# Expert down products in fp32r halves, loop bounds read into registers once, merged matrix split inside the context attention

## The reference, cut to what matters

```python
x = x + tanh(g_xattn[0]) * lag_attention(layernorm(x), ctx, ctx)          # part 1
x = x + tanh(g_ffn[0])   * experts(layernorm(x), gate_w, u, g, d)          # parts 2 and 3
x = x + tanh(g_xattn[1]) * cross_attention(layernorm(x), ctx, Wq, bq, Wk, bk)  # part 4
x = x + tanh(g_ffn[1])   * quantised_ffn(layernorm(x), ...)                # part 5

# experts: 2048 rows of 1024, 16 experts of 112 inner units, two experts for each row
w = weights of the two chosen experts of each row
gate_out, up_out = x @ g.T, x @ u.T          # split by expert
h = silu(gate_out) * up_out
out = einsum('bei,hei,be->bh', h, d_r, w)    # the down product

# cross attention
Q, K = text @ Wq.T + bq, ctx @ Wk.T + bk
out = softmax(Q @ K.T / 32) @ ctx
```

## Time and profile before

| | |
|---|---|
| median of 3 runs | 1354.48 us (1353.6 to 1355.89) |
| the profiled execution, own time | 1356.5 us |
| its span, from the first instruction to the last | 1354.8 us |
| instructions | 20940 |
| PE busy | 1239.7 us, 92% of the span |
| DVE, ACT, POOL busy | 783.7, 513.5, 573.0 us |
| experts: gate and up of tile 0 to the last down product | 598 to 839 us |

### The profile page before, as it was taken

One profiled execution on the slowest core, in us unless ns is written; L12 is line 12 of the kernel. 1 busy time (PEld: TensorE's weight loads), 2 busy tenths in 40 slices (PEclk: granted clock), 3 DMA queues, 4 the chain that ended last, 5 costly groups with the idle time before them and its releaser, 6 DMA issues. The chain is left out here.

```text
span 1354.8 us, 20940 instructions
## 1 busy us (share of the span) xinstructions
PE 1239.7 (92%) x6442; PEld 846.7 (62%) x6442; DVE 783.7 (58%) x2026; ACT 513.5 (38%) x939; POOL 573.0 (42%) x931
## 2 busy tenths in 40 slices
PE   4799999999878999999999998999999999968886
PEld 2354544445435954458888786988888898635443
DVE  3889999998963680015433333444554443369885
ACT  2555545454423400023322222232222322168894
POOL 5667877777642001013221222523212231068884
PEclk8999999999988899999999999999999999879998
DMA  5211212302004502227778874535333331131111
GB/s 197 92 64 32 93 62 96 138 31 109 0 1 149 224 1 84 70 85 246 265 240 283 273 233 161 187 94 128 114 103 124 96 101 54 62 70 47 62 62 78
DMA packets 52481, 156.25 MB, mean 115 GB/s; under 512 B 5952, under 2 KB 16192, under 8 KB 52288
## 3 DMA queue, kind: packets, MB, share of 16 engines
q1 hardware_dynamic: 39152, 113.46, 23.6%
q0 software_dynamic: 13264, 41.95, 10.8%
HBM read 112.93 MB, written 45.61 MB: 117 GB/s over the span
## 5 line engine op out<-in xcount | busy, mean ns | idle before, releaser
L1210 PEld LDWEIGHTS ex_bank<-ex_xT,ex_gu 128*112 128x112 f32 x1248 | 140.4, 177 | 24.3 <-issue 23.3
L1210 PE MATMUL ex_bank<-ex_xT,ex_gu 128*112 128x128 f32 x1248 | 143.6, 273 | 2.0 <-issue 1.0
L44 PE MATMUL xa_bank<-fT_high,M_hi 128*128 128x256 f32 x512 | 144.0, 281 | 0.0
L46 PE MATMUL xa_bank<-fT_high,M_lo 128*128 128x256 f32 x512 | 143.0, 279 | 0.0
L45 PE MATMUL xa_bank<-fT_low,M_hi 128*128 128x256 f32 x512 | 142.9, 279 | 0.0
L52 PE MATMUL la_bank<-la_osum,la_tab 128*128 128x512 f32 x256 | 120.8, 617 | 24.1 <-POOL la_osum L291 23.7
L291 POOL TENSOR_TENSOR la_osum<-la_oprod 128x512 f32<-128x512 f32 x64 | 80.1, 1273 | 73.7 <-DVE la_oprod L479 73.7
L1074 POOL TENSOR_TENSOR ex_small<-listed,ex_small 128x1 int32<-128x1 int32 x42 | 15.4, 368 | 223.7 <-DVE Wk L1152 223.5
L52 PEld LDWEIGHTS la_bank<-la_osum,la_tab 128*128 128x128 f32 x256 | 47.7, 196 | 86.4 <-issue 48.6
L44 PEld LDWEIGHTS xa_bank<-fT_high,M_hi 128*128 128x128 f32 x512 | 96.7, 189 | 0.3
L46 PEld LDWEIGHTS xa_bank<-fT_high,M_lo 128*128 128x128 f32 x512 | 96.7, 189 | 0.0
(11 more groups left out here) (284 smaller groups left out, 2853.4 us busy)
## 6 DMA issues: line engine op xcount, KB each, us to landing
produced<-Wk SPq DMA_DIRECT2D x39, 512.0 KB
ex_gu<-in_gate_up SPq DMA_DIRECT2D x16, 896.0 KB
X<-in_x SPq DMA_DIRECT2D x8, 1024.0 KB, 7.4
la_v_raw<-in_ctx SPq DMA_DIRECT2D x16, 512.0 KB, 4.0
produced<-la_zeros SPq DMA_DIRECT2D x16, 512.0 KB, 4.7
normal<-rt_xn SPq DMA_DIRECT2D x16, 512.0 KB, 5.4
fT<-in_ctx_T SPq DMA_DIRECT2D x8, 1024.0 KB, 5.7
xa_f<-in_ctx SPq DMA_DIRECT2D x8, 1024.0 KB, 4.8
```

The source lines that it names most:

```text
L44: pe.matmul(out, a[0], b[0], start=first, stop=False)
L46: return pe.matmul(out, a[1], b[0], start=False, stop=last)
L1210: m = pe.matmul(bank[half][0:INTER, 0:P], gu[:, slot, at:at + INTER], xT[:, k, :], start=(k == 0), stop=(k == KD - 1))
```

## The change

Three things are edited.

First, the down product is made from halves. ACT makes `dn_hi`, an fp32r copy of the expert's whole `dn` (`down_high`, 112 x 1024), and DVE makes `dn - dn_hi` in the place of `dn` (`down_low`). Both run once for each expert, ahead of its first tile. `dn_hi` has one buffer. For each tile DVE makes `h_hi` (fp32r) and `hT` (float32) from silu and up, waits for its own `hT`, and makes `h_lo = hT - h_hi`. PE makes the down product as `h_hi*dn_hi + h_hi*dn_lo + h_lo*dn_hi`: six fp32r matmuls of 512 columns. It waits for `dn_lo` ahead of them and for `h_lo` ahead of the last two.

Second, ACT and DVE no longer have twelve tiles written out and one loop, but one loop for each expert. They read all 17 values of `first_tile` into registers ahead of the first (`edge`). PE and SP read two for each expert as before.

Third, `M_hi` and `M_lo` are no longer made beside the tiles but in `context_attention`: three blocks at its start and five after `row_high(0)` on ACT, `row_low(0)` on DVE. `g_block(0, m)` waits for its block. The split of the first `fT` moves to the starts of experts 4 to 7.

```diff
+        dn_low = nc.alloc_sbuf_tensor_at("ex_dn_low", [INTER, SLOTS, D], F32R, offset=at)   # the place of dn
@@ experts, sync
+                    sp.wait_ge(s["dn_lo"], e + 1)
                     load(e + SLOTS)
@@ experts, scalar
-            total = act.value_load(first_tile[0:1, EXPERTS:EXPERTS + 1], min_val=1, max_val=MAX_TILES)
+            def down_high(e):
+                act.wait_ge(w_in[e % SLOTS], 32 * (e // SLOTS + 1))
+                at_least(act, s["dn_lo"], e)
+                act.activation(dn_hi, dn[:, e % SLOTS, :], ACT.Copy).then_inc(s["dn_hi"], 1)
...
-            for g in range(BESIDE):
-                tile(g)
-            with act.Fori(BESIDE, total) as g:
-                tile(g)
+            edge = [act.value_load(first_tile[0:1, e:e + 1], min_val=min(e, 1), max_val=MAX_TILES) for e in range(EXPERTS + 1)]
+            for e in range(EXPERTS):
+                down_high(e)
+                beside(e)
+                with act.Fori(edge[e], edge[e + 1]) as g:
+                    tile(g)
@@ experts, vector (edge and the loops as on ACT)
+            def down_low(e):
+                dve.wait_ge(s["dn_hi"], e + 1)
+                dve.tensor_tensor(dn_lo(e % SLOTS), dn[:, e % SLOTS, :], dn_hi.bitcast(F32), ALU.subtract).then_inc(s["dn_lo"], 1)
...
-                dve.tensor_tensor(hT[:], sg[:], bank[1][0:INTER, 0:P], ALU.mult).then_inc(s["hT_ready"], 1)
+                dve.tensor_tensor(h_hi, sg[:], bank[1][0:INTER, 0:P], ALU.mult).then_inc(s["hT_ready"], 1)
+                dve.tensor_tensor(hT[:], sg[:], bank[1][0:INTER, 0:P], ALU.mult).then_inc(s["hT_whole"], 1)
+                dve.wait_ge(s["hT_whole"], g + 1)
+                dve.tensor_tensor(h_lo, hT[:], h_hi.bitcast(F32), ALU.subtract).then_inc(s["hT_lo"], 1)
@@ experts, tensor
+                    pe.wait_ge(s["dn_lo"], e + 1)
                     for i in range(2):
-                        m = pe.matmul(bank[4 + i][:], hT[:], dn[:, slot, i * 512:(i + 1) * 512], start=True, stop=True)
+                        half = slice(i * 512, (i + 1) * 512)
+                        pe.matmul(bank[4 + i][:], h_hi, dn_hi[:, half], start=True, stop=False)
+                        pe.matmul(bank[4 + i][:], h_hi, dn_lo(slot)[:, half], start=False, stop=False)
+                    pe.wait_ge(s["hT_lo"], g + 1)
+                    for i in range(2):
+                        m = pe.matmul(bank[4 + i][:], h_lo, dn_hi[:, i * 512:(i + 1) * 512], start=False, stop=True)
@@ context_attention, scalar
+            for m in range(3):
+                merged_high(m)
             act.wait_ge(s["gate_in"], 32)
...
             row_high(0)
+            for m in range(3, KD):
+                merged_high(m)
@@ context_attention, vector
+            for m in range(3):
+                merged_low(m)
...
             row_low(0)
             for i in range(4):
+                merged_low(3 + i)
                 combine(0, i)
+            merged_low(7)
@@ context_attention, tensor
+                if b == 0:
+                    pe.wait_ge(s["m_lo"], m + 1)
```

More of the change, by code:

```diff
@@ L990, in _, with experts @@
                 merged_product(pe, bank[n % 4][:], W, n).then_inc(s["m_pe"], 1)
-def experts(nc, gate_up, down, normal, listed, produced, first_tile, W, M32, M, features_T, fT, fT_parts):
+def experts(nc, gate_up, down, normal, listed, produced, first_tile, W, M32, M, features_T, fT, fT_parts, halves):
     with ExitStack() as ctx:
@@ L1016, in experts, with dn_lo @@
         ident = W[1][:, 6, 0:P]
+        h_hi, h_lo, dn_hi = (tensor[:] for tensor in halves)
+        def dn_lo(slot):
+            return dn_low[:, slot, :]
         names = """one consts current rows_ready rows_held turned xT_act xT_dve gate_done up_half up_done silu_done hT_ready down_done
-                   m_pe m_out m_hi fT_in fT_hi y_act y_dve y_st all_stored""".split()
+                   m_pe m_out m_hi fT_in fT_hi y_act y_dve y_st all_stored dn_hi dn_lo hT_whole hT_lo""".split()
         s = {n: sem(n) for n in names}
@@ L1120, in tile @@
                 rows_out(g + 1)
[L1121 to L1127, removed]
                 act.wait_ge(s["down_done"], g + 1)
@@ L1177, in tile @@
                 dve.tensor_copy(y[:, 512:1024], bank[5][:]).then_inc(s["y_dve"], 1)
[L1178 to L1181, removed]
+            edge = [dve.value_load(first_tile[0:1, e:e + 1], min_val=min(e, 1), max_val=MAX_TILES) for e in range(EXPERTS + 1)]
+            for e in range(EXPERTS):
+                down_low(e)
+                beside(e)
+                with dve.Fori(edge[e], edge[e + 1]) as g:
+                    tile(g)
         @block.tensor
@@ L1347, in _, with merged_high @@
         def _(act):
+            def merged_high(m):
+                part = (slice(None), slice(None), slice(m * P, (m + 1) * P))
+                act.activation(M[0][part], M32[part], ACT.Copy).then_inc(s["m_hi"], 1)
             def features_high(b):
@@ L1912, in quarter @@
                     return nc.alloc_sbuf_tensor_at(name, [P, KD, L], dt, offset=at + i * 2 * D * 4)
+                halves = [nc.alloc_sbuf_tensor_at(name, [INTER, cols], F32R, offset=at + first * 4)
+                          for name, first, cols in (("h_high", 6 * D + P, P), ("h_low", 6 * D + 2 * P, P), ("down_high", 7 * D, D))]
                 xn = W[1][:, 0:2, :]
```

34 lines of the change are left out of this document (20 added, 14 removed).

## The result

The changed kernel takes 1374.81 us (median of 4 runs, 1374.09 to 1378.49) and the kernel before 1355.18 on the same chip (4 runs, 1353.6 to 1357.38). The ratio is 1.0149, 95% interval 1.0126 to 1.0173: slower by 19.6 us, where 1373 (1361 to 1383) was forecast. The profiled execution of after has a span of 1376.8 us and a time of its own of 1378.49, against 1354.8 and 1356.5 before.

A forecast was written before the change was run, and what follows sets the result against it. PE's list was taken to bound both the experts' stage and the context attention. Terms -0.7 + 11.5 + 8.0 = 18.8 us slower gave 1375 us on the profiled execution, 1373 us at the median, range 1361 to 1383.

The forecast's parts named there:

- products, where no change follows: Experts' tiles not followed by a change of expert: 24 x 0.37 = 8.9 us saved (7.4 to 10.3).
- changes with PE's reads: At 15 changes of expert, bound reads bring the next gate product 0.35 us later: 5.2 us lost (3 to 6).
- chain behind the copy of y: At six changes, late copy of y, then down_high, down_low and h, delay the down product: 3 us lost (0 to 6).
- reads ahead of the first tile: 17 reads at 0.72 us on DVE delay the first down product from 602.60 to 611.6: 9.0 us lost.
- clock behind them: After PE's stop at the first tile, five us of work run at half pace: 2.5 us lost (1.7 to 3.4).
- context attention: Merged-matrix halves made in this stage: block 2 of G waits 6.0 us, lower clock 2.0 more, 8.0 us lost.
- The product: Down product: six fp32r matmuls at 0.224 us take 1.34 us against 1.72, saving 0.37 us a tile (0.31 to 0.43).
- the rival in which the reads overlap: Ahead of the first tile: 17 reads at 0.3 us each, first down product 1.7 us late, 1363 us; chance 0.16.
- The merged matrix: Context attention: five ACT blocks delay G by 3.5 us, POOL's late identity adds 2.5, the lower clock 2.0 (0 to 2.5).
- The rival in which entering a loop costs 1 us: At changes of expert: ACT and DVE each lose 1 us entering a loop, some 22 us, 1395 us; chance 0.09.
- The range: Whole kernel: bounds taken singly give 1362 to 1382 us; with overlapping reads inside, 1361 to 1383 holds some 0.8.

The follow-up runs named there:

- experiment 9: The changed kernel with a second buffer for y and nothing else; 1369.25 us, ratio 1.0113 to the kernel before.
- 11: The kernel before with two buffers for y and PE's 17 reads of the edges spread through the merged products; 1347.04 us, ratio 0.996.
- experiment 6: The changed kernel with ACT, DVE and PE reads moved earlier, identity ahead of gathers, fewer M_hi blocks ahead of G, and two buffers for y; 1337.39 us, ratio 0.9875.
- experiment 10: The kernel before with two buffers for y and nothing else; 1352.66 us, ratio 1.0002.
- experiments 2 and 3: The changed kernel with one of five M_hi blocks left ahead of G's first copy (1372.14 us), or with POOL's identity matrix ahead of its gathers (1372.37 us).
- 7: The kernel of experiment 5 with the next expert's down-weight halves made beside the first tile of this one, still one y; 1347.49 us, ratio 0.9946.
- experiment 5: The changed kernel with ACT, DVE and PE reads moved earlier, identity ahead of gathers, one M_hi block ahead of G's first copy, one y; 1357.71 us, ratio 1.0022.
- experiment 4: The changed kernel with PE's 17 reads spread two by two behind its merged products, none at a change of expert; 1375.01 us, ratio 1.0158.

## Why the prediction was right, step by step

All terms from the profiled executions. The predicted sum of 18.8 us stands beside 22.0 us in the span and 19.6 in the medians. The terms are divided as the prediction divided them: at a change of expert the saving of the product is inside the term of the change.

| term | predicted | measured | from |
|---|---|---|---|
| products, where no change follows | -8.9 | -7.6 | 135.2 - 2.8 (9, less the clock below) - 140.0 (before) |
| changes with PE's reads | +5.2 | +4.8 | 99.7 (9) - 94.9 (before) |
| chain behind the copy of y | +3.0 | +9.1 | 244.0 - 234.9 (after, 9) |
| reads ahead of the first tile | +9.0 | +7.6 | 12.00 - 4.45 |
| clock behind them | +2.5 | +2.8 | 8.55 - 5.76 |
| context attention | +8.0 | +7.3 | 513.7 - 506.4 |

They sum to 23.9 us; the stage's first gate product came 2.1 us earlier in after's run than in before's, at a place that the change does not touch, and the last T lies 0.2 us further from B. That gives the 22.0.

- **The product.** 0.33 us in a tile, at the low end of the 0.31 to 0.43, and partly by luck. The two steps taken for it do not come to that: the six products and the hand-over take 1.47 us from T to S where 1.34 was reckoned (0.32 us from the first to the second, 728.98 to 729.30, then 0.23, against the 0.224 I took between two rows), so that step saves 0.25 us and not 0.37. The other 0.08 us lie between S and the next T (4.37 us before, 4.29 after), where the prediction saw nothing.
- **PE's reads.** At a change the next gate product comes 0.36 us later than before (2.26 us from T to S in the mean of the 15 in experiment 9, 1.90 before), where 0.35 was said. With experiment 10 as the kernel before, whose changes take 96.9 us, the term is 2.8 us and not 4.8, just below the 3 to 6. Taken by themselves, products of halves are worth 12.2 us in the 38 tiles (11 and 6), and the reads cost 0.87 us at a change of after and 0.24 to 0.37 before.
- **The chain.** This term was mis-sized by a factor of three and lies outside its own range of 0 to 6 us. The chain's length was about right (3.4 us said, 3.05 measured, 3.66 where features are split too), and so was the place where it begins. Wrong was what I made of it: I counted late copies in the trace of before (six changes; it has five at 3.65 us or more, the next is at 2.90) and kept them as they were. But a tile shorter by 0.33 us leaves the store that much less, and the store does not get shorter: from its issue to a copy that starts more than 2.3 us after T it is 5.2 us in the mean before and 5.1 in after. So in after seven changes and two distances inside an expert have a copy 3.7 us or more behind T and a product held back by it. 6.9 of the 9.1 us are at changes (106.6 against 99.7), 2.2 elsewhere, and some 1.7 of the whole are the 3.4 us at the lower clock from 822.1 on. In the traces of experiments 2 and 3, which have the same experts' stage, the term is 8.0 and 7.2. At a change it needs both, the late copy and the halves behind it: the second buffer takes all of the term away (9), and halves made ahead, tried on the kernel of experiment 5 alone, take 13.1 us of its 22.5 (7, 5 and 6).
- **The reads ahead of the first tile.** 0.63 us a read where 0.72 was taken, beginning 2.1 us earlier with the stage; the first down product at 608.06 and not at 611.6, and 7.6 us late. Mechanism, stop and clock as predicted; the rival in which the reads overlap is out. The Trainium skill, page "Runtime: NRT & Kernel Launch", section "Instruction fetch mechanics", gives some 200 ns for each register of a TENSOR_LOAD (the page has them as loads from HBM). Here, with the values in SBUF, the load alone takes 0.30 us and a read of one value 0.63 from start to start, so its figure is too low for these reads.
- **The merged matrix.** A stop of 5.85 us (6.0 predicted), POOL later by some 2.2 us (2.5), the lower clock behind it: 5.4 us of work at 0.50, 2.7 us lost where 2.0 (0 to 2.5) was said. Stop and clock make 8.5 us, and the total is 7.3 because before had lost some 1.1 us that after did not: its first block of G began at 848.34 with the clock low until 850.50, after's at 863.03 as it rose. The whole term is in the first of the eight batch items: from B to the first block of G of the second item takes 36.98 us before and 44.30 in after, and each of the next six steps 41.37 in both. Experiments 2 and 3 show that both causes are real, each worth about 4 us of the stop. POOL's step of 0.19 us took 1.07 while VectorE's subtraction ran (862.16, below). The Trainium skill, page "SBUF — State Buffer", section "SBUF: two separate sides", says that an operation of VectorE with two inputs in SBUF and one of GpSimd that reads SBUF exclude each other for the whole instruction. The trace agrees with that: the step of 1.07 us ends at 863.2, as the second of VectorE's three subtractions does.

```profile
860.07 0.19 POOL L1341 TENSOR_TENSOR xa_small_u<-xa_small_u 128x1 uint32<-128x1 uint32 x1
...
860.73 3.58 DVE L1453 TENSOR_TENSOR M_lo<-M,M_hi 128x1024 fp32r<-128x1024 f32 x3 [4.55 <-ACT M_hi L1376]
...
862.16 1.07 POOL L1341 TENSOR_TENSOR xa_small_u<-xa_small_u 128x1 uint32<-128x1 uint32 x1
```

- **The rival in which entering a loop costs 1 us** is out: the changes of after need nothing beyond PE's reads and the store, and once both are gone a change takes the same 5.76 us as any tile (experiment 6).
- **The range.** The terms at all their low ends give about 1360 us and at all their high ends about 1384, so the 1362 to 1382 that the prediction calls its bounds is narrower than they allow. The result lies inside either.

Five of the six terms came within 1.4 us. The chain was off by 6 us, and that the median still falls within 1 us of the forecast's difference is in part luck: the stage began 2.1 us earlier, and the profiled execution of after lies 3.7 us above its median, that of before 1.3 above the median of its four runs.

## What to carry to other kernels

A wait that an engine off the path has (here ScalarE for a store, 72.5 us in all) is slack that a faster path uses up: before shortening the loop, ask whether the wait's own length shrinks with it, and if not, double its buffer first. The single y cost the kernel before nothing and the changed one 9 us of its stage (3 to 6 in the medians), and with TensorE's reads out of the way some 20. Reads of values into registers cost 0.56 to 0.63 us each in a row on one engine's list; they belong where that engine waits anyway, and the kernel with products of halves, early reads and two y beats the kernel before by 1.25%.

## What the runs showed that I had not expected

- Taking away work from the bound engine (experiment 4) gave nothing at all: -7.1 us at the changes, +5.0 in the other tiles, and the clock low for 3.4 us at two further places behind the longer stops.
- The stage is not bound by the rate of the DMA engines although each tile's store, gather and weights pass through them: with two y they moved 256 GB/s at a busy share of 0.76, with one 225 at 0.68.
- An fp32r product of 512 columns follows another after 0.23 us at full clock (729.30 to 729.53), twice the 0.12 of 256 columns; at the lower clock the same step is 0.43 us (608.65 to 609.08 in after). A float32 record of 512 columns takes 0.43 us at full clock, 1.72 us for four.
- Each of 17 reads in a row takes 0.30 us for the load and 0.18 for its register operation on VectorE, yet the reads start 0.63 us apart; on ScalarE 0.56.
